# Second output stage of a decoder layer: its weights prepared during cross attention, low parts on GpSimd, scatters spread over two tiles

## Chip, cores and metric

One core of one Trainium2 chip. The metric is the device time of one execution in microseconds; the kernel before takes 2526.17 us, the median of 3 runs (2526.06 to 2526.66). All times below come from these runs and from one profiled execution of the kernel before.

## What is computed

A pre-norm decoder layer in float32 over 16 sequences of 112 tokens (1792 tokens of width 512): self attention with compressed keys and values, cross attention to 375 context tokens per sequence, then a mixture of experts.

```
x = x + self_attention(layernorm(x))              # 16 heads
x = x + cross_attention(layernorm(x), ctx) @ Wo.T # 16 heads of 128; Wo is (512, 2048)
x = x + moe(layernorm(x))

moe: probs = softmax(x @ classifier.T)            # 12 choices, 8 of them real experts
     top 2 of probs + bias; weight 1.5 * probs
     out  = sum of weight * (silu(x @ gate.T) * (x @ up.T)) @ down.T over chosen experts
          + x * (sum of the weights of the 4 choices without an expert)
```

The change touches the product with `Wo` that follows cross attention, what is computed with it (residual, norm, choice of experts, list of the tokens of each expert), and the cross attention ahead of it.

## The kernel before

The kernel runs stages one after the other; each is a block in which every engine has its own program in order, and a barrier stands between blocks. Every float32 product is made of three TensorE products: a value is split into a high part (rounded, made by a copy) and a low part (value minus high part), and hi*hi, hi*lo and lo*hi are summed in PSUM (`mm3`, L75 to L77).

`cross_attention` (block at 1024 to 1957 us) loops over 16 batches of four steps. In a step TensorE scores a quarter of the heads of batch b, weighs and projects keys and values of batch b+1; GpSimd's `project` adds and scales the next batch's keys and makes a low part of the context (L1957 to L1969); VectorE takes maxima and divides (L2220, L2227); ScalarE takes exponentials. The last batch has no next one to project, so GpSimd has nothing to do in it.

`cross_output` (1960 to 2228 us) is the second output stage. It goes over 14 tiles of 128 tokens. For tile t:

- SP loads the 16 heads' outputs in 4 chunks of 4 heads (L1486) and the residual (L1489), two tiles ahead, and stores the normed rows (L1494). A chunk is loaded when the low part of the tile before has been made of the same buffer (`o_lo_ready`).
- ScalarE makes the high part `o_hi` (`high`, L1562) when TensorE has used that chunk of the tile before; VectorE makes the low part `o_lo` (`low`, L1607).
- TensorE: `project` (4 chunks of 12 products, 128x512), `turn` (L1728, four transposes of the normed tile), `count` (L1747, L1748), `route` (12 small products). Its order for tile t is: project chunks 0 and 1 of t+1, turn t, project chunks 2 and 3 of t+1, count t-1, route t.
- VectorE: `norm` (residual added L1615, statistics L262 and L265, scaled L269), low part, `route(t-1)` (L1631 to L1649, the choice of two experts), `turn`, low part, `locate(t-2)` (L1659 to L1665, the places of the tile's tokens in the experts' lists), two low parts.
- GpSimd: `root(t)` (L275, L277: the variance to the power -0.5, which `norm` waits for), then `scatter(t-2)`: two indirect DMAs (L1540), one for the first and one for the second choice of each token. Each waits until the one before has landed (`scattered`), the first also for `locate(t-2)`.

`count(t-1)` on TensorE waits for `locate(t-2)` and `route(t-1)` of VectorE. `locate(t)` waits for the scatters of t-2.

Before the first tile the weights `Wo` come in 16 loads of one head each (L1499, 256 KB) through 8 buffers, ScalarE makes their high parts (L1587), VectorE their low parts (L1689), and the projection of tile 0 waits for each head (`w_lo_ready`). The classifier, the bias and the zeros of the lists are loaded ahead of them (L1476 to L1479). After the block comes `experts` (from 2228 us).

Of the kernel before, what the change touches and what calls it, by code (L numbers as in the profile page):

```python
# [11 lines left out]
ALU = mybir.AluOpType  # L12
# [1374 lines left out]
def cross_output(nc, oT, w_src, res, router, keep):  # L1387
# [4 lines left out]
    with ctx:  # L1392
# [3 lines left out]
        RAW = 8  # L1396
        w_raw = sb('w_raw', [P, RAW, D])
        w_hi = sb('w_hi', [P, H, D], F32R)
        w_lo = sb('w_lo', [P, H, D], F32R)
# [15 lines left out]
        w_in = [ctx.sem(f'w_loaded{i}') for i in range(RAW)]  # L1415
        w_hi_ready = ctx.sem('w_hi_ready')
        w_lo_ready = ctx.sem('w_lo_ready')
# [55 lines left out]
        def _(sp):  # L1473
            for i in range(2):
                y_put[i].open(sp)
            sp.dma_start(cls[:, :, :], cls_src).then_inc(r_src, 16)  # L1476
# [4 lines left out]
            def load(t, h, par, chunks=range(NQ), residual=True):  # L1481
                cols = bass.ds(t * P, P)
                for c in chunks:
                    if not isinstance(t, int) or t:
                        wait(sp, o_lo_ready, t, c - NQ)
                    sp.dma_start(o_raw[:, c, :, :], oT[:, c * HQ:(c + 1) * HQ, cols]).then_inc(o_in[c].sem, 16)  # L1486
                if residual:
                    wait(sp, added, t, -2)
                    sp.dma_start(r_in[par][:, :], res[cols, :]).then_inc(r_loaded[par].sem, 16)  # L1489
# [23 lines left out]
        def _(pool):  # L1513
            identity(pool, ident[:, :], id_ready)
            pool.iota(iota_i[:, :], pattern=[[1, TOTAL]], base=0, channel_multiplier=0).then_inc(id_ready, 1)
            pool.wait_ge(id_ready, 3)
            pool.tensor_copy(iota[:, :], iota_i[:, :]).then_inc(id_ready, 1)
            pool.memset(fill[:, :], 0).then_inc(zeroed, 1)
# [12 lines left out]
            exponent(pool, minus_half[:, :], half_ready)  # L1531

            def scatter(t, par):
                for c in range(2):
                    if c == 0:
                        wait(pool, p_step, t, 4)
                    if c or not isinstance(t, int) or t:
                        wait(pool, scattered, t, c - 1)
                    carry(pool, t, ticks)
                    pool.indirect_dma_start(tokens, bass.IndirectOffsetOnAxis(ap=dest_i[par][:, c:c + 1], axis=0), id_i[par][:, :], None).then_inc(scattered.sem, 16)  # L1540
            pool.wait_ge(list_ready, 16)
            for par in range(2):
                layer.root(pool, par, minus_half)

            def pair(h):
                for par in range(2):
                    layer.root(pool, h * 2 + par, minus_half)
                    scatter(h * 2 + par - 2, par)
            pair(1)
            with pool.Fori(2, TT // 2) as h:  # L1550
                pair(h)
            scatter(TT - 2, 0)
            scatter(TT - 1, 1)
            pool.wait_ge(scattered.sem, scattered.at(TT - 1, 1))

        @block.scalar
        def _(act):
# [16 lines left out]
            def body(t, h, par, ahead=True):  # L1574
                if ahead:
                    high(t + 2, 0)
                if not (isinstance(t, int) and t == 0):
                    route(t - 1)
                turn(t, h, par)
                if ahead:  # L1580
                    high(t + 2, 1)
                    high(t + 2, 2)
                if ahead:
                    high(t + 2, 3)
            for h in range(H):
                act.wait_ge(w_in[h % RAW], 16 * (h // RAW + 1))
                act.activation(w_hi[:, h, :], w_raw[:, h % RAW, :], ACT.Copy).then_inc(w_hi_ready, 1)  # L1587
                if h % HQ == 0:
                    high(0, h // HQ)
            for c in range(NQ):  # L1590
                high(1, c)
# [10 lines left out]
        def _(dve):  # L1602
            added.open(dve)

            def low(t, c):
                wait(dve, o_hi_ready, t, c)
                dve.tensor_tensor(o_lo[:, c, :, :], o_raw[:, c, :, :], o_hi[:, c, :, :], ALU.subtract).then_inc(o_lo_ready.sem, 1)  # L1607
# [59 lines left out]
            def body(t, h, par, ahead=True):  # L1667
                norm(t, h, par)
                if ahead:
                    low(t + 2, 0)  # L1670
# [3 lines left out]
                if ahead:  # L1674
                    low(t + 2, 1)
                if not (isinstance(t, int) and t < 2):
                    locate(t - 2, par)
                if ahead:
                    low(t + 2, 2)
                    low(t + 2, 3)  # L1680
# [6 lines left out]
            for h in range(H):  # L1687
                dve.wait_ge(w_hi_ready, h + 1)
# [1052 lines left out]
```

## Time and profile before

| | |
|---|---|
| Median of 3 runs | 2526.17 us (2526.06 to 2526.66) |
| Profiled execution | 2526.26 us, span 2524.6 us, mean granted TensorE clock 0.939 |
| TensorE matmul busy | 2182.0 us (86% of the span) |
| VectorE, ScalarE, GpSimd busy | 1332.6, 1030.3, 785.3 us (53%, 41%, 31%) |
| Low parts of the outputs on VectorE (L1607) | 56 of 0.691 us |
| Scatters on GpSimd (L1540) | 28, from 2020.3 to 2223.3 us |

The profile has a row per instruction: its engine, line, what it writes and reads, and the idle time of the engine before it with the instruction that ended it. The span is the time from the first to the last instruction; the execution's time is a little longer. A projection's row lasts 0.39 us at full clock, but the engine starts the next one before it ends, so distances of starts are read rather than durations.

### The profile page before, as it was taken

How to read it: one execution, taken by the hardware profiler on the slowest of the kernel's cores; microseconds unless marked ns; L12 is line 12 of the kernel's file. 1: busy time of each engine (PE TensorE's matmuls, PEld its weight loads, DVE VectorE, ACT ScalarE, POOL GpSimd, SP SyncE). 2: the span in 40 equal slices, each digit the busy share in tenths (PEclk: the TensorE clock that was granted, in tenths of full speed). 3: DMA queues.
4: the chain of work that ended last, by engine and by line, in shares of the span. 5: the costliest groups of instructions: out<-in, count | busy, mean ns of one | idle time of the engine just before them, and what ended most of it. 6: DMA issues, size and time to landing. Idle time of an engine off the chain costs nothing. (4 is left out here: it accounts for less than half of the span.)

```text
span 2524.6 us, 35645 instructions
## 1 busy us (share of the span) xinstructions
PE 2182.0 (86%) x10448; PEld 1661.2 (66%) x10448; DVE 1332.6 (53%) x2902; ACT 1030.3 (41%) x2200; POOL 785.3 (31%) x818
## 2 busy tenths in 40 slices
PE   5689999985898998599999999999998789638991
PEld 3588888864676776466666666666664667527771
DVE  3535555556667667354545454544544655534553
ACT  2323333334444344255555555555555311125660
POOL 2400000003555556432323232323230021145664
PEclk8899999997899999799999999999999999769995
DMA  7621221142344444212222222222211643154336
GB/s 283 166 73 37 63 66 36 33 164 88 107 126 136 134 121 147 87 54 65 73 67 67 64 57 64 57 70 66 74 32 37 193 97 94 38 193 132 104 104 191
DMA packets 291586, 243.77 MB, mean 97 GB/s; under 512 B 148034, under 2 KB 255026, under 8 KB 288562
## 3 DMA queue, kind: packets, MB, share of 16 engines
q1 hardware_dynamic: 271426, 194.38, 26.2%
q10 hardware_dynamic: 13584, 30.02, 3.3%
q0 software_dynamic: 6496, 18.37, 2.6%
q8 instruction: 41, 0.67, 0.1%
q14 instruction: 39, 0.32, 0.0%
HBM read 149.31 MB, written 93.42 MB: 96 GB/s over the span
## 5 line engine op out<-in xcount | busy, mean ns | idle before, releaser
L2220 DVE TENSOR_REDUCE ca_down<-ca_ps_s 112x1 f32<-112x487 f32 x256 | 164.6, 661 | 309.8 <-PE ca_ps_s L2035 307.3
L1963 POOL TENSOR_TENSOR ca_k<-ca_k 125x512 f32<-125x512 f32 x64 | 81.2, 1269 | 554.3 <-DVE ca_k L2205 554.3
L2035 PE MATMUL ca_ps_s<-ca_kT,ca_qT 128*112 128x487 f32 x512 | 230.5, 572 | 0.8 <-issue 0.8
L2124 ACT ACTIVATE ca_prob<-ca_ps_s,ca_down 112x487 f32<-112x487 f32 x256 | 169.8, 666 | 135.2 <-DVE ca_down L2220 131.1
L75 PE MATMUL out_ps_y<-out_w_hi,out_o_hi 128*128 128x512 f32 x448 | 191.8, 428 | 37.1 <-DVE out_w_lo L1288 19.0
L2051 PE MATMUL ca_ps_o<-ca_pT,ca_v 125*128 125x448 f32 (+1 forms) x512 | 203.2, 539 | 0.6 <-ACT ca_pT L2131 0.6
L75 PE MATMUL ca_ps_p<-ca_w_hi,ca_c_hi 128*125 128x512 f32 x384 | 174.1, 453 | 23.1 <-POOL ca_c_lo L1957 23.1
L76 PE MATMUL out_ps_y<-out_w_lo,out_o_hi 128*128 128x512 f32 x448 | 183.8, 410 | 0.0
L77 PE MATMUL out_ps_y<-out_w_hi,out_o_lo 128*128 128x512 f32 x448 | 183.5, 410 | 0.0
L2051 PEld LDWEIGHTS ca_ps_o<-ca_pT,ca_v 125*128 125x128 f32 (+1 forms) x512 | 97.1, 190 | 100.9 <-issue 100.1
L76 PE MATMUL ca_ps_p<-ca_w_lo,ca_c_hi 128*125 128x512 f32 x384 | 153.8, 400 | 0.0
L77 PE MATMUL ca_ps_p<-ca_w_hi,ca_c_lo 128*125 128x512 f32 x384 | 153.6, 400 | 0.0
L2042 PEld LDWEIGHTS ca_ps_t<-ca_ident,ca_prob 112*125 112x125 f32 x1024 | 131.6, 188 | 24.5 <-DVE ca_prob L2227 11.8
L599 POOL COPY sa_val<-lat_v 112x128 f32<-112x128 f32 (+1 forms) x64 | 18.9, 296 | 409.9 <-PE sa_ps_o L656 409.6
L2042 PE MATMUL ca_ps_t<-ca_ident,ca_prob 112*125 112x112 f32 x1024 | 132.9, 272 | 7.4 <-DVE ca_prob L2227 6.8
L75 PEld LDWEIGHTS out_ps_y<-out_w_hi,out_o_hi 128*128 128x128 f32 x448 | 90.4, 202 | 60.1 <-issue 33.6
L2131 ACT ACTIVATE ca_pT<-ca_ps_t 125x448 f32<-125x448 f32 x256 | 125.2, 543 | 4.3 <-PE ca_ps_t L2042 4.3
L2227 DVE TENSOR_SCALAR ca_prob<-ca_prob,ca_inv 112x487 f32<-112x487 f32 x256 | 121.2, 473 | 9.2 <-DVE ca_inv L2225 0.2
L75 PE MATMUL sa_ps_q<-sa_xh,qf_hi 128*128 128x448 f32 (+1 forms) x256 | 115.5, 451 | 8.4 <-DMA sa_xl<-x0T_lo 8.4
L2035 PEld LDWEIGHTS ca_ps_s<-ca_kT,ca_qT 128*112 128x112 f32 x512 | 80.4, 177 | 60.5 <-issue 60.5
L2202 DVE TENSOR_TENSOR ca_k<-ca_ps_p,ca_tab 125x512 f32<-125x512 f32 x64 | 44.3, 692 | 137.8 <-ACT ca_sq L2104 137.8
L707 ACT ACTIVATE sa_ov<-sa_ps_o 128x448 f32<-128x448 f32 x64 | 35.0, 547 | 196.9 <-PE sa_ps_o L656 187.8
(291 smaller groups left out, 5591.3 us busy)
## 6 DMA issues: line engine op xcount, KB each, us to landing
self_outT<-sa_ov SPq DMA_DIRECT2D x64, 224.0 KB, 2.4
out_o_raw<-self_outT SPq DMA_DIRECT2D x56, 256.0 KB, 3.0
cross_qT<-out_qt SPq DMA_DIRECT2D x56, 256.0 KB, 2.4
ca_qT<-cross_qT SPq DMA_DIRECT2D x64, 224.0 KB, 2.8
cross_outT<-ca_ov SPq DMA_DIRECT2D x64, 224.0 KB, 3.0
out_o_raw<-cross_outT SPq DMA_DIRECT2D x56, 256.0 KB, 3.5
ffn_raw<-in_expert_w SPq DMA_DIRECT2D x8, 1536.0 KB
ca_c_first<-in_ctxT SPq DMA_DIRECT2D x15, 750.0 KB, 5.1
```

Source lines behind the costliest of these rows:

```text
L75: pe.matmul(out, a_hi, b_hi, start=start, stop=False)
L76: pe.matmul(out, a_hi, b_lo, start=False, stop=False)
L77: return pe.matmul(out, a_lo, b_hi, start=False, stop=stop)
L1963: pool.tensor_tensor(k1[0:m, :], k1[0:m, :], k2[0:m, :], ALU.add).then_inc(k_added.sem, 1)
L2035: pe.matmul(ps_s[j % 2][:, :], qT[i % 2][:, j, :], kT[par][:, i, :], start=True, stop=True).then_inc(scored.sem, 1)
L2042: mm = pe.transpose(ps_t[j % 2][0:CT, t, :], prob[j][:, t * CT:(t + 1) * CT], ident[0:S, 0:S])
L2051: mm = pe.matmul(ps_o[:, :, :], v[par][0:M[t], t, i * HD:(i + 1) * HD], pT[i % 2][0:M[t], t, :, :], start=(t == 0), stop=(t == 3))
L2124: act.activation(prob[j][:, 0:KV], ps_s[j % 2][:, :], ACT.Exp, bias=down[:, j:j + 1], accum_out=total[:, j:j + 1]).then_inc(exped.sem, 1)
L2131: act.activation(pT[i % 2][0:CT, :, j, :], ps_t[j % 2][0:CT, :, :], ACT.Copy).then_inc(pT_ready.sem, 1)
L2202: dve.tensor_tensor(h4(k1[0:m, :]), h4(ps), over_heads(tab[par][0:m, i, 0, :], HQ), ALU.mult)
L2220: dve.tensor_reduce(down[:, j:j + 1], ps_s[j % 2][:, :], AX.X, ALU.max, negate=True).then_inc(maxed.sem, 1)
L2227: dve.tensor_scalar(prob[j][:, 0:KV], prob[j][:, 0:KV], inv[:, j:j + 1], None, ALU.mult).then_inc(probs.sem, 1)
```

## The change

- `CrossOutputWeights` holds the weights of the second output stage in two buffers of 16 heads at the right end of SBUF, with the raw weights in the place of the low parts. It is made before `cross_attention` and handed to it as `next_w`, then to `cross_output` as `ahead_of`.
- ScalarE issues four loads of 4 heads (1 MB) in batch 0 of cross attention, one at the head of each step. GpSimd splits one head (copy, then subtraction) at the end of each step of batches 1 and 14, and two in each step of batch 15.
- In `cross_output` the loads and splits of the weights, their semaphores and TensorE's waits on them are gone. SP's first issues are the outputs of tile 0. GpSimd's start is reordered around the low parts of tile 0.
- The low parts of the outputs are made by GpSimd.
- A tile's two scatters stand in different tiles of GpSimd's order: `root(t)`, second scatter of t-3, two low parts of t+2, first scatter of t-2, two low parts of t+2.
- ScalarE's `route(t-1)` stands before its first high part of t+2.

```diff
+class CrossOutputWeights(ExitStack):
+    def __init__(self, nc, w_src):
+        super().__init__()
+        self.src = w_src
+        with nc.sbuf_tensor("out2_w_raw", [P, H, D], F32, side="right") as self.w_raw:
+            pass
+        self.w_lo = self.enter_context(nc.sbuf_tensor("out2_w_lo", [P, H, D], F32R, side="right"))
+        self.w_hi = self.enter_context(nc.sbuf_tensor("out2_w_hi", [P, H, D], F32R, side="right"))
...
+    def load(self, eng, c):
+        heads = slice(c * HQ, (c + 1) * HQ)
+        eng.dma_start(self.w_raw[:, heads, :], self.src[:, heads, :]).then_inc(self.w_in[c], 16)
+
+    def split(self, pool, h):
+        pool.wait_ge(self.w_in[h // HQ], 16)
+        pool.tensor_copy(self.w_hi[:, h, :], self.w_raw[:, h, :]).then_inc(self.hi_ready, 1)
+        pool.wait_ge(self.hi_ready, h + 1)
+        pool.tensor_tensor(self.w_lo[:, h, :], self.w_raw[:, h, :], self.w_hi[:, h, :], ALU.subtract)
...
 cross_output, SP
+            load(0, 0, 0)
             sp.dma_start(cls[:, :, :], cls_src).then_inc(r_src, 16)
...
-            for h in range(H):
-                if h >= RAW:
-                    sp.wait_ge(w_lo_ready, h - RAW + 1)
-                sp.dma_start(w_raw[:, h % RAW, :], w_src[:, h, :]).then_inc(w_in[h % RAW], 16)
-                if h % HQ == 0:
-                    load(0, 0, 0, [h // HQ], h == H - HQ)
...
 cross_output, GpSimd
+            def low(t, c):
+                wait(pool, o_hi_ready, t, c)
+                carry(pool, t, ticks)
+                pool.tensor_tensor(o_lo[:, c, :, :], o_raw[:, c, :, :], o_hi[:, c, :, :], ALU.subtract).then_inc(o_lo_ready.sem, 1)
+
             identity(pool, ident[:, :], id_ready)
+            pool.memset(fill[:, :], 0).then_inc(zeroed, 1)
+            exponent(pool, minus_half[:, :], half_ready)
+            for c in range(NQ):
+                low(0, c)
...
+            def body(t, par, ahead=True):
+                early = lambda n: isinstance(t, int) and t < n
+                layer.root(pool, t, minus_half)
+                if not early(3):
+                    scatter(t - 3, 1, 1 - par)
+                if ahead:
+                    low(t + 2, 0)
+                    low(t + 2, 1)
+                if not early(2):
+                    scatter(t - 2, 0, par)
+                if ahead:
+                    low(t + 2, 2)
+                    low(t + 2, 3)
...
 cross_output, ScalarE
             def body(t, h, par, ahead=True):
+                if not (isinstance(t, int) and t == 0):
+                    route(t - 1)
                 if ahead:
                     high(t + 2, 0)
-                if not (isinstance(t, int) and t == 0):
-                    route(t - 1)
                 turn(t, h, par)
...
 cross_output, VectorE: low() and its calls removed
-            def low(t, c):
-                wait(dve, o_hi_ready, t, c)
-                dve.tensor_tensor(o_lo[:, c, :, :], o_raw[:, c, :, :], o_hi[:, c, :, :], ALU.subtract).then_inc(o_lo_ready.sem, 1)
...
 cross_attention, GpSimd
             def step(b, h, i, par, more):
                 if more:
                     project(b + 1, i, 1 - par)
+                if isinstance(b, int) and b:
+                    first = {1: i, B - 2: HQ + i, B - 1: 2 * (HQ + i)}[b]
+                    for head in range(first, first + (2 if b == B - 1 else 1)):
+                        next_w.split(pool, head)
...
 cross_attention, ScalarE
+                if isinstance(b, int) and b == 0:
+                    next_w.load(act, i)
                 exp(b, i, 0)
```

## Rows read from the trace of the kernel before

**Rows 1.** view of windows: us, busy us (instructions) per engine, clock, DMA share, GB/s.
```profile
1095.00:1895.00 800.00, 800.00 (x3434) 539.41 (x3434) 398.31 (x970) 414.87 (x957) 243.71 (x213) 1.00 0.23 62
...
1960.00:1985.00 25.00, 15.40 (x56) 11.07 (x57) 16.02 (x25) 15.12 (x24) 2.48 (x15) 0.80 0.90 279
...
2060.00:2100.00 40.00, 33.89 (x153) 27.43 (x152) 21.10 (x76) 7.89 (x18) 7.52 (x11) 0.89 0.38 87
```

**Rows 2.** waits, 2000 to 2200 us: engine line <- releaser: us, times, longest.
```profile
DVE out_yn L269 <- POOL out_mean_var L277: 59.8, 12, 7.2
...
PE out_ps_x L1728 <- DVE out_yn L269: 20.3, 9, 5.0
```

**Rows 3.** timeline of TensorE: start, us, line, operation, count, idle before.
```profile
1989.05 0.66 PE L1728 MATMUL out_ps_x<-out_ident,out_yn 128*128 128x128 f32 x4
...
2015.03 0.60 PE L1728 MATMUL out_ps_x<-out_ident,out_yn 128*128 128x128 f32 x4
...
2060.17 0.39 PE L75 MATMUL out_ps_y<-out_w_hi,out_o_hi 128*128 128x512 f32 x1
2060.40 0.39 PE L76 MATMUL out_ps_y<-out_w_lo,out_o_hi 128*128 128x512 f32 x1
...
2064.16 0.63 PE L75 MATMUL out_ps_y<-out_w_hi,out_o_hi 128*128 128x512 f32 x1
...
2080.12 0.65 PE L1728 MATMUL out_ps_x<-out_ident,out_yn 128*128 128x128 f32 x4 [2.25 <-DVE out_yn L269]
...
2180.83 0.60 PE L1728 MATMUL out_ps_x<-out_ident,out_yn 128*128 128x128 f32 x4
...
2193.61 1.12 PE L1728 MATMUL out_ps_x<-out_ident,out_yn 128*128 128x128 f32 x4 [5.00 <-DVE out_yn L269]
```

**Rows 4.** timeline of GpSimd, one tile of the second output stage.
```profile
2054.37 1.48 POOL L1540 DMA_INDIRECT tokens_of_experts<-out_id_i,out_dest_i  x1 [9.18 <-DVE out_dest_i L1665]
2060.39 0.96 POOL L1540 DMA_INDIRECT tokens_of_experts<-out_id_i,out_dest_i  x1 [4.54 <-DMA tokens_of_experts<-out_id_i,out_dest_i]
2061.37 0.25 POOL L275 TENSOR_SCALAR out_mean_var<-out_mean_var 128x1 f32<-128x1 f32 x1
```

**Rows 5.** timeline, start of the stage: SP's first issue, TensorE's first projection.
```profile
1960.86 0.36 SPq L1476 DMA_DIRECT2D out_cls<-in_clsT  x1
...
1968.47 0.77 PE L75 MATMUL out_ps_y<-out_w_hi,out_o_hi 128*128 128x512 f32 x1 [12.12 <-DVE out_o_lo L1607]
```

**Rows 6.** single lines (duration ns min/median/max), then timelines of GpSimd and VectorE.
```profile
L1957 POOL TENSOR_TENSOR ca_c_lo<-ca_c_first,ca_c_hi x48: 1148/1171/2742, 1027.0 to 1876.6; 128x500 fp32r<-128x500 f32 x48
...
2274.23 4.62 POOL L2388 TENSOR_TENSOR ffn_w_lo<-ffn_raw,ffn_w_hi 128x2048 fp32r<-128x2048 f32 x1 [5.44 <-ACT ffn_w_hi L2483]
...
2278.19 1.75 DVE L2586 TENSOR_TENSOR ffn_w_lo<-ffn_raw,ffn_w_hi 128x1024 fp32r<-128x1024 f32 x1 [1.90 <-ACT ffn_w_hi L2483]
...
2287.84 1.22 DVE L2586 TENSOR_TENSOR ffn_w_lo<-ffn_raw,ffn_w_hi 128x1024 fp32r<-128x1024 f32 x1 [1.92 <-ACT ffn_w_hi L2483]
```

**Rows 7.** timelines: VectorE's route and locate, first and last; a high part of ScalarE.
```profile
2064.03 0.16 DVE L1633 RECIPROCAL out_small<-out_small 128x1 f32<-128x1 f32 x1 [0.50 <-ACT out_prob L1572]
...
2070.03 0.17 DVE L1665 CAST out_dest_i<-out_dest 128x2 uint32<-128x2 f32 x1
...
2070.67 0.63 ACT L1562 ACTIVATE out_o_hi<-out_o_raw 128x512 fp32r<-128x512 f32 x1 [2.09 <-PE out_ps_y L77]
```

**Rows 8.** landing of L1486 and of L1540.
```profile
DMA to landing us min/median/max: 2.8/3.5/7.7
...
DMA to landing us min/median/max: 2.5/4.3/6.9
```

**Rows 9.** like loads of ScalarE; waits 1100 to 1956 us; last batch on TensorE.
```profile
L907 ACTq DMA_DIRECT2D out_wq_raw<-in_xwqT x4: 547/644/691, 552.3 to 558.9; - x4
...
ACT ca_prob L2124 <- DVE ca_down L2220: 127.6, 124, 1.3
...
1920.67 1.51 PE L2042 MATMUL ca_ps_t<-ca_ident,ca_prob 112*125 112x112 f32 x8 [1.44 <-DVE ca_prob L2227]
```

More of the change, by code:

```diff
@@ L1475, in _, with load, store @@
                 y_put[i].open(sp)
+            def load(t, h, par):
+                cols = bass.ds(t * P, P)
+                for c in range(NQ):
+                    if not isinstance(t, int) or t:
+                        wait(sp, o_lo_ready, t, c - NQ)
+                    sp.dma_start(o_raw[:, c, :, :], oT[:, c * HQ:(c + 1) * HQ, cols]).then_inc(o_in[c].sem, 16)
+                wait(sp, added, t, -2)
+                sp.dma_start(r_in[par][:, :], res[cols, :]).then_inc(r_loaded[par].sem, 16)
+            def store(t, h, par):
+                cols = bass.ds(t * P, P)
+                wait(sp, normed, t)
+                sp.dma_start(rows_n[cols, :], yn[par][:, :]).then_inc(y_put[par].sem, 16)
+            load(0, 0, 0)
             sp.dma_start(cls[:, :, :], cls_src).then_inc(r_src, 16)
@@ L1479, in _ @@
             sp.dma_start(tokens.rearrange('(p n) o -> p (n o)', p=P), fill[:, :]).then_inc(list_ready, 16)
[L1481 to L1489, printed above, removed]
-            def store(t, h, par):
-                cols = bass.ds(t * P, P)
-                wait(sp, normed, t)
-                sp.dma_start(rows_n[cols, :], yn[par][:, :]).then_inc(y_put[par].sem, 16)
-            for h in range(H):
-                if h >= RAW:
-                    sp.wait_ge(w_lo_ready, h - RAW + 1)
-                sp.dma_start(w_raw[:, h % RAW, :], w_src[:, h, :]).then_inc(w_in[h % RAW], 16)
-                if h % HQ == 0:
-                    load(0, 0, 0, [h // HQ], h == H - HQ)
             load(1, 0, 1)
@@ L1541, in _, with scatter @@
[L1541 to L1554, printed above, removed]
+            def scatter(t, c, par):
+                if c == 0:
+                    wait(pool, p_step, t, 4)
+                if c or not isinstance(t, int) or t:
+                    wait(pool, scattered, t, c - 1)
+                carry(pool, t, ticks)
+                pool.indirect_dma_start(tokens, bass.IndirectOffsetOnAxis(ap=dest_i[par][:, c:c + 1], axis=0), id_i[par][:, :], None).then_inc(scattered.sem, 16)
@@ new lines, in _ @@
+            pool.wait_ge(list_ready, 16)
+            for c in range(NQ):
+                low(1, c)
+            for t in range(4):
+                body(t, t % 2)
+            with pool.Fori(2, TT // 2 - 1) as h:
+                for par in range(2):
+                    body(h * 2 + par, par)
+            for par in range(2):
+                body(TT - 2 + par, par, ahead=False)
+            scatter(TT - 3, 1, 1)
+            for t in range(TT - 2, TT):
+                for c in range(2):
+                    scatter(t, c, t % 2)
@@ L1556, in _ @@
+            wait(pool, scattered, TT - 1, 1)
         @block.scalar
@@ L2685, in build @@
         keep = acc, oh, place, weight, run, rows_n, tokens
-        cross_output(nc, o2T, xwoT, x1, (clsT, bias), keep)
+        with cross_out_w:
+            cross_output(nc, o2T, cross_out_w, x1, (clsT, bias), keep)
         experts(nc, expert_w, *keep, rows_y, out_rows)
```

66 lines of the change are left out of this document (16 added, 50 removed).

## Prediction

> **What bounds the kernel now.** I read the table of windows first [rows 1], because shares over the whole span mix stages. From 1095 to 1895 us, cross attention, TensorE is busy 800.00 of 800.00 us at granted clock 1.00: nothing that only relieves another engine can gain there. The second output stage (1960 to 2228 us) is different. It opens with 15.40 busy us in 25, at a DMA share of 0.90, and from 2060 to 2100 TensorE is idle 6 of 40 us and the granted clock is 0.89.
>
> Next, who waits for whom in that stage [rows 2]. VectorE waits 59.8 us for GpSimd's root of the variance, and TensorE 20.3 us for the normed tile behind it. Only the second wait is a loss by itself; the first leads to it.
>
> The timeline of TensorE gives the price [rows 3]. `turn(t)` (L1728) is the tile's mark. It starts at 1989.05 (t=0), 2015.03 (2), 2080.12 (6), 2180.83 (12) and 2193.61 (13). The first two intervals together are 25.98 us, 12.99 each, with no idle time named before them; that is TensorE's own work. From t=6 to t=12 an interval is 16.79 us (100.71 in six). At t=6 2.25 us of it are idle time before `turn`, and behind such a wait a projection lasts 0.63 us (2064.16) instead of 0.39 (2060.17). That is the lower of the two clock levels, 1.2 GHz against 2.4: 512 columns then take 0.43 us from start to start, where 2060.17 to 2060.40 shows 0.23. What 16.79 has over 12.99 + 2.25, 1.55 us, is about eight such projections.
>
> The timeline of GpSimd names the cause [rows 4]. The scatter of a tile's first choice starts at 2054.37, the second can start only when the first has landed, at 2060.39, and `root` (L275) stands behind it at 2061.37. The variance had been ready long before. So the serial pair of scatters in front of `root` sets the pace, and TensorE pays for it twice, in idle time and in clock.
>
> **The change, part by part.** The sum is made against the profiled execution: 2526.26 us, of which 2524.60 are span and 1.66 around it; it stands 0.09 us above the median of 2526.17.
>
> *Start of the stage.* Removed from the stage: 16 weight loads, 16 splits on ScalarE and VectorE, and their waits. SP's first issue is at 1960.86 and the first projection at 1968.47 [rows 5]. Afterwards SP's first issue is the first chunk of the outputs. That load takes 2.8 us at best [rows 8], so it lands at 1963.7; ScalarE's high part 0.63 [rows 7], GpSimd's low part 1.2 (below), two handovers of 0.1: the first projection starts about 1965.7. The tile needs 72 projections before `turn(0)`: 7 at 0.43 and 65 at 0.227, 17.8 us, so `turn(0)` at 1983.4 rather than 1989.05: **-5.7 us**. Bounds: -2.8 (only the earlier start, the rest of the 20.6 us kept) and -7.1 (full clock at once). The identity, the zeros for the list and `exponent` are moved ahead of the low parts, the other tables behind them. The tables are eleven small instructions; at 0.2 us each (an estimate from `root`'s first one, 0.25 in rows 4) they end near 1971.6, behind four low parts that end near 1969.3, and tile 1's first low part is wanted only when the fourth chunk ends, at 1978. On SP the classifier, bias and list loads go behind five loads, some 2.5 us later, wanted by GpSimd near 1969: covered, and 1 us each if not.
>
> *A tile in the steady state.* VectorE loses four low parts; GpSimd takes them at about 1.2 us each (1.171 median for 128x500 [rows 6]), 4.8 us. With two scatters of about 1.0 and a `root` of 0.9 GpSimd holds 7.7 us of work per tile, below 13.1. What decides is the order. Let 0 be the end of the projections of tile t. ScalarE's last high part is ready at 0.9, the last low part stands before `root` until 2.2, VectorE's add and statistics, two passes over 512 columns at 0.7 (L2586 does 1024 in 1.22 [rows 6]) and a short one, are ready at 2.1; `root` ends at 3.15, the normed tile at 3.8. TensorE comes to `turn(t)` after count and route (1.6, what 12.99 leaves beside 48 projections and `turn`) and 24 projections (5.45), at 7.1. So the new wait in front of `root` has a margin of 3.3 us. Queued behind it on GpSimd: scatter of t-3's second choice (first one issued some 6 us earlier in the tile before), two low parts, scatter of t-2's first choice, two low parts. These low parts are wanted by TensorE some 8 us later, and they free the buffers for SP's loads of t+3, which land 3.5 us after issue [rows 8] and are wanted a tile later. ScalarE's `route`, now ahead of its first high part, holds that until 4.6, when the chunk is just used: nothing.
>
> On VectorE, `route(t-1)` and `locate(t-2)` follow. Their row distance, 2064.03 to 2070.20, is 6.17 us with one low part in it [rows 7]: 5.5 without. Starting at 4.5 they would end at 10.0, or 10.3 since `turn`'s result comes at 8.3. TensorE asks for them in `count` at 13.1. With nothing late the tile is TensorE's own again. I take 13.1 us, from the two undisturbed intervals of 12.99 on average (a little more, since `count` is missing in the first). Twelve intervals, t=0 to t=12: 157.2 instead of 191.78 (1989.05 to 2180.83): **-34.6 us**. Bounds: -35.9 (12.99 each) and -23 (14.1, see the rivals).
>
> *Does GpSimd's work hold VectorE back?* The subtraction L2586, 128x1024 with both inputs in SBUF, takes 1.22 us where GpSimd only issues a DMA, and 1.75 us where it starts at 2278.19 while GpSimd's subtraction runs until 2278.85 [rows 6]: it begins in effect when that ends (0.66 + 1.09). So I let `route` and `locate` be held by one low part each, up to 1.2 us: the chain ends at 11.7, still 1.4 before `count`. The Trainium skill, "SBUF — State Buffer", section "SBUF: two separate sides", speaks against this change: the two engines share a pair of SBUF ports as an exclusive lock, so a VectorE instruction with two SBUF inputs waits for the whole GpSimd instruction. By that rule the move could cost the lock rival's time below, without it the move is free; these rows agree with it.
>
> *Last tiles.* From t=12 to t=13 there is no further tile to project. Before: 12.78 us, 5.00 of them waiting for `root` behind two scatters [rows 3]. After: 0.6 + 5.45 to the end of the projections, 3.7 for the norm: 9.75. **-3.0 us** (bounds -4 and 0). From `turn(13)` on nothing changes: six scatters, each behind the landing of the last, to the end of the stage. In both versions six remain after `turn(13)`, the tenth tile's second one now standing before them behind `root`. **0**, within 2 us either way, as landings are 2.5 to 6.9 us.
>
> *Cross attention.* Four loads of 1 MB are issued by ScalarE in batch 0, 0.64 us each by the like loads L907 [rows 9]. ScalarE waits there for the maximum anyway (127.6 us in 124 times, about 1.0 each), and the DMA share is 0.23, so 4 MB over four steps of 14 us are covered: 0, with +2 as the other bound. GpSimd gets 16 splits of a copy (no row shows one of that size: more than the 0.25 of one column in rows 4, less than the 1.2 of a subtraction; I take 0.7) and a subtraction of 1.2: 2 us each. Batches 1 and 14 have one per step of about 14 us (933 us for 64 steps), behind the step's own work, and GpSimd is busy only 243.71 of 800 us [rows 1]: 0. In batch 15 eight stand in a row, some 16 us. TensorE is not full there, it waits for VectorE's `prob` (1.44 us at 1920.67 [rows 9]). Each first scaling of a pair can be held by up to 1.2 us, over one and a half steps: 0 to +6 if the clock falls too, I take **+1.5 us**. What covers the splits otherwise is TensorE's own work.
>
> Sum: 2526.26 - 5.7 - 34.6 - 3.0 + 1.5 = **2484.5 us**.
>
> **The rivals.** *The lock.* Were VectorE held three or four times a tile, its chain would end near 14.1 and `count` would wait 1 us in each tile: 12 x 1.0 = +12, 2496.5 us. For it: rows 6. Against: two of the four low parts fall where VectorE waits or reads PSUM.
>
> *The scatters stay serial.* Each still waits for the landing of the one before, two per tile. Their spacing within a tile is 6.0 us in rows 4, and may be as long as the longest landing, 6.9 [rows 8], twice which is 13.8, above 13.1. If the shorter tile crowds the DMA queues and spacing rises to 7.0, the period is 14.0: +11, 2495.5 us. Against it: the median landing of all 28 is 4.3 us [rows 8].
>
> *Slower than before.* The same chain decides from a period of 16.6 us on, a spacing of 8.3: 12 x 16.6 = 199 = 191.78 + 7.2, what the start, the last tile and cross attention save together. At 9 us the period is 18, 12 x 18 = 216, and the time 2484.5 + 58.8 = 2543 us. Against it: the longest landing seen is 6.9 us.
>
> *A wait takes the place of the one removed.* If `root` is as late as now because of the low parts before it (ScalarE's fourth high part late, for example), the period stays near 16 (191.78 us for twelve) and the last tile keeps its wait: 2526.26 - 5.7 + 1.5 = 2522 us, within 0.2%.
>
> *Cross attention pays more*, with the bound of +6: 2489 us.
>
> **How the numbers follow.** Forecast within 2479 to 2490: 0.62. Lock: 0.12. Serial scatters at 14: 0.12. Cross attention +6: 0.06. Period unchanged: 0.04. Slower: 0.04. All but the last two are faster by over 0.2% (5 us, about what a measurement of this kernel can tell from no change): 0.92; within it 0.04; slower 0.04. The low end adds the good bounds (-1.4, -1.3, -1, -1.5, and -2 of the last landings): 2477.3. The high end is either rival of +12 with +4.5 of cross attention: 2501.
>
> **What the profile after would show.** First L75 on `out_ps_y` at 1965 to 1966 plus what cross attention lost; `turn` every 13.0 to 13.3 us with no idle time before it and clock 1.00 from the second tile on; `root` no longer behind a landing; GpSimd's low part 1.2 us, stretched VectorE instructions beside it. The lock would show as TensorE's `count` waiting for `dest_i`; the serial chain as GpSimd's second scatter waiting for DMA in each tile and `turn` waiting for `yn`. The prediction is wrong if the interval of `turn` is over 14, or if batch 15 grows by more than 6 us.

## The result

The changed kernel takes 2491.23 us (median of 6 runs, 2486.19 to 2497.86); the kernel before, run beside it, 2524.34 (2521.97 to 2526.66). The ratio is 0.9872, 95% interval 0.9854 to 0.9891: 33 us faster. The forecast was 2484.5, range 2477 to 2501; the median lies in that range, 1.2 us above the band of 2479 to 2490 that had the chance 0.62. The profiled execution took 2492.17 us, 34.09 below the one of before.

First the view of windows, in the three stretches of [rows 1]: us, busy us (instructions) per engine, clock, DMA share, GB/s.

```profile
1095.00:1895.00 800.00, 800.00 (x3431) 539.71 (x3430) 397.97 (x970) 413.93 (x955) 258.26 (x230) 1.00 0.24 65
1960.00:1985.00 25.00, 15.49 (x55) 12.38 (x56) 1.37 (x4) 5.27 (x9) 11.97 (x23) 0.80 0.51 146
2060.00:2100.00 40.00, 40.00 (x204) 33.32 (x204) 24.20 (x77) 9.64 (x21) 24.61 (x24) 1.00 0.46 114
```

Cross attention carries GpSimd's splits and TensorE is as full as before. In the last line TensorE has lost its 6 idle us of 40 and the granted clock is 1.00, not 0.89. GpSimd has gone from 7.52 to 24.61 busy us. The waits from 2000 to 2200 us, against [rows 2]: engine line <- releaser: us, times, longest.

```profile
POOL tokens_of_experts L1560 <- DVE out_dest_i L1691: 36.3, 11, 5.6
DVE out_yn L269 <- POOL out_mean_var L277: 22.9, 12, 2.8
...
PE out_ps_c L1755 <- DVE out_dest_i L1691: 11.6, 3, 5.6
...
PE out_ps_x L1736 <- DVE out_yn L269: 1.8, 1, 1.8
```

VectorE waits 22.9 us for `root` instead of 59.8, TensorE 1.8 us for `yn` instead of 20.3. Of the three waits of `count` for `dest_i` two (5.56 and 5.19 us) lie behind the last turn, where nothing is left to project; the third, 0.82 us, is in the long tile below.

The turns in TensorE's timeline, against [rows 3]: start, us, line, operation, count, idle time before.

```profile
1989.02 0.60 PE L1736 MATMUL out_ps_x<-out_ident,out_yn 128*128 128x128 f32 x4
...
2055.87 0.49 PE L1736 MATMUL out_ps_x<-out_ident,out_yn 128*128 128x128 f32 x3
...
2069.33 0.60 PE L1736 MATMUL out_ps_x<-out_ident,out_yn 128*128 128x128 f32 x4
...
2109.71 0.60 PE L1736 MATMUL out_ps_x<-out_ident,out_yn 128*128 128x128 f32 x4
...
2125.80 0.60 PE L1736 MATMUL out_ps_x<-out_ident,out_yn 128*128 128x128 f32 x4
...
2152.71 0.49 PE L1736 MATMUL out_ps_x<-out_ident,out_yn 128*128 128x128 f32 x3
2162.41 0.67 PE L1736 MATMUL out_ps_x<-out_ident,out_yn 128*128 128x128 f32 x4 [1.80 <-DVE out_yn L269]
```

From `turn(0)` to `turn(12)` it is 163.69 us instead of 191.78. Ten of the twelve intervals are 13.45 or 13.46, the first is 13.01, and one, from 2109.71, is 16.09. So two things differ from the forecast of 13.1: every tile is 0.36 us longer, and one tile 2.6 more. The experiments are about these two, and about which part of the change brought what.

How the 34.09 us come together, both profiled executions: up to the end of cross attention +3.28 (3.24 of it are there at 1079.82 us, and the first of the new loads is issued at 1079.08); end of cross attention to the first projection -2.24; to `turn(0)` -1.07; twelve intervals -28.09; t=12 to 13 -3.08; `turn(13)` to the experts' first matmul -1.54; the rest -1.35. The stretches with unchanged code vary from profile to profile: cross attention ended between 1953.0 and 1964.5, the experts' stage took 273.7 to 282.8, the kernel before 2511.89 to 2531.00 in all. The usual intervals of `turn` repeat to 0.1 us, so the readings below go by them; the long ones do not repeat.

### The profile page after: what moved, and what is told of

Read it like the earlier page. It is cut to its first block and busy times, and to the rows that moved or that the text cites. A ratio compares the mean times of both kernels' runs of the same rounds, so it can differ in the third digit from the quotient of the medians.

```text
span 2490.5 us, 35704 instructions
## 1 busy us (share of the span) xinstructions
PE 2181.5 (88%) x10448; PEld 1664.9 (67%) x10448; DVE 1309.4 (53%) x2830; ACT 1020.9 (41%) x2184; POOL 887.9 (36%) x906
```

## Experiments: which part brings what

All kernels are read in the same way. "Start" is SP's first issue in the stage to `turn(0)`, "twelve" is `turn(0)` to `turn(12)`, "spacing" the mean distance from start to start of the projections at full clock, worked out from TensorE's timeline. "w-o" is the start of `w_hi` in its partition less that of `o_hi`, in bytes, modulo 512 (in all kernels it is the same for `w_lo` and `o_lo`). The last column is the ratio to the kernel before, run beside it. The last three kernels had one run each (2487.68, 2481.57 and 2488.29 us), so only their intervals are read; starts, spacings and intervals are always those of one profiled execution.

| kernel | low parts | scatters | weights | w-o | spacing | usual interval | twelve | start | ratio |
|---|---|---|---|---|---|---|---|---|---|
| before | VectorE | pair | in stage | 0 | 0.228 | 12.8 to 18.2 | 191.78 | 28.19 | 1 |
| changed | GpSimd | apart | ahead | 416 | 0.2345 | 13.46 | 163.69 | 24.72 | 0.9872 |
| a2_after_again | GpSimd | apart | ahead | 416 | 0.234 | 13.46 | 166.48 | 24.59 | 0.9896 |
| e1_apart_only | VectorE | apart | in stage | 0 | 0.228 | 13.16 | 158.14 | 27.79 | 0.9879 |
| e4_weights_only | VectorE | pair | ahead | 416 | 0.234 | 13.0 to 18.0 | 192.86 | 22.75 | 0.9971 |
| e2_low_dve | VectorE | apart | ahead | 416 | 0.2345 | 13.46 | 161.07 | 22.74 | 0.9844 |
| e3_pair | GpSimd | pair | ahead | 416 | 0.234 | 13.0 to 18.7 | 203.49 | 24.73 | 1.0039 |
| e5_pad32 | GpSimd | apart | ahead | 384 | 0.232 | 13.37 | 160.05 | 24.66 | 0.9858 |
| e8_place | VectorE | apart | ahead | 0 | 0.228 | 13.17 | 157.77 | 23.51 | 0.9842 |
| e12_place_gps | GpSimd | apart | ahead | 0 | 0.228 | 13.16 | 169.78 | 24.25 | 0.9873 |
| e10_out_shift | VectorE | apart | ahead | 448 | 0.233 | 13.41 | 160.55 | 23.89 | - |
| e11_w_shift | VectorE | apart | ahead | 0 | 0.228 | 13.17 | 157.60 | 23.56 | - |
| e13_both_shift | VectorE | apart | ahead | 0 | 0.228 | 13.16 | 157.66 | 22.37 | - |

(e6_warm, e8_place with extra projections, stands in its own section.)

**The scatters apart, alone.** The kernel before with this in place of `scatter(t-2)`:

```diff
 layer.root(pool, t, minus_half)
-scatter(t - 2, par)
+if not isinstance(t, int) or t > 2:
+    scatter(t - 3, 1, 1 - par)
+scatter(t - 2, 0, par)
```

> The kernel before with one part of the change only: GpSimd's order per tile is root(t), scatter of the second choice of t-3, scatter of the first choice of t-2. Weights are loaded and split inside the stage, low parts stay on VectorE, as before. Theory (the pair of scatters ahead of root set the pace, the rest is cover): the interval of turn falls from 16.79 us to 13.0 to 13.5, t=12 to t=13 from 12.78 to 9.8, the start of the stage is unchanged: 28 to 34 us less than before plus 3, so 31 to 37 us faster, ratio 0.985 to 0.988. If in addition the projections come at 0.227 us here (0.235 in the changed kernel), the slower spacing belongs to the moved weights or to GpSimd's low parts, and the interval is about 13.0. Rival (low parts on VectorE are the next bound, so both parts are needed): the interval stays above 14.5 and the gain is under 25 us. Rival (GpSimd's lock costs in the changed kernel): no interval over 14 here after tile 2, and the times of the runs lie within 1 us of each other.

Measured: 2489.43 us (2488.20 to 2495.11), ratio 0.9879 (0.9847 to 0.9910). Two tiles on TensorE:

```profile
2019.04 0.60 PE L1732 MATMUL out_ps_x<-out_ident,out_yn 128*128 128x128 f32 x4
2032.19 0.60 PE L1732 MATMUL out_ps_x<-out_ident,out_yn 128*128 128x128 f32 x4
2045.35 0.60 PE L1732 MATMUL out_ps_x<-out_ident,out_yn 128*128 128x128 f32 x4
```

and GpSimd in one tile, against [rows 4]:

```profile
2071.07 1.09 POOL L1539 DMA_INDIRECT tokens_of_experts<-out_id_i,out_dest_i  x1 [1.75 <-DMA tokens_of_experts<-out_id_i,out_dest_i]
2078.88 1.40 POOL L1539 DMA_INDIRECT tokens_of_experts<-out_id_i,out_dest_i  x1 [6.72 <-DVE out_dest_i L1669]
2081.31 0.22 POOL L275 TENSOR_SCALAR out_mean_var<-out_mean_var 128x1 f32<-128x1 f32 x1 [1.03 <-DVE out_mean_var L265]
```

`root` now waits for VectorE's variance, 1.03 us, and for no landing. This one part takes 33.6 us off the twelve intervals and 3.2 off the last tile, all that was forecast for the whole change there (34.6 and 3.0), and with this alone the kernel is as fast as the changed one. The low parts on VectorE are no bound: the rival that both parts are needed falls. The four runs spread over 6.9 us though GpSimd makes no low parts here.

**The weights ahead, alone.**

```diff
 # the changed kernel, low parts back on VectorE
-scatter(t - 3, 1, 1 - par)
 scatter(t - 2, 0, par)
+scatter(t - 2, 1, par)
```

> One part of the change alone: the weights are loaded and split beside cross attention and the stage starts with the outputs' chunks; the low parts stay on VectorE and a tile's two scatters stay together, ahead of the next root, as before. Theory: SP's first issue to the first projection falls from 7.6 to 4.5, first projection to turn(0) from 20.5 to 18.2, so 5 us less at the start; the twelve intervals stay what the pair of scatters makes them, 190 to 195 us, a little more by the slower projections (12 x 0.3 = 3.6 us where TensorE sets the pace, nothing where the scatters do); sum 2516 to 2522, 2 to 7 us faster than before. Rival (weights at the right end cost in every tile what the start gains): within 2 us of before.

Measured: 2514.34 us (2510.18 to 2520.50, 10 runs), ratio 0.9971 (0.9956 to 0.9987), a little below the 2516 to 2522 expected. The start is 5.4 us shorter, what the prediction had put down (5.7); the twelve intervals are 192.86, as long as before.

**The scatters together again, low parts on GpSimd.**

```diff
 # the changed kernel, GpSimd
-scatter(t - 3, 1, 1 - par)
 low(t + 2, 0); low(t + 2, 1)
 scatter(t - 2, 0, par)
+scatter(t - 2, 1, par)
 low(t + 2, 2); low(t + 2, 3)
```

> The changed kernel with both scatters of a tile together again: root, two low parts, both scatters of t-2, two low parts. Theory (apart is what counts): GpSimd stands at the second scatter until the first has landed (about 5 us), and the low parts behind it and the next root come late: interval 15.5 to 17, time 2515 to 2530. Rival (the low parts between are room enough, or the weights ahead are what counts): interval 13.5 to 14, time 2490 to 2497.

Measured: 2531.74 us, ratio 1.0039 (1.0025 to 1.0054), slower than before and above the 2515 to 2530 expected; the usual interval is near 18 us, not 15.5 to 17, and the twelve together take 203.49 us. GpSimd's timeline shows why:

```profile
2073.05 1.09 POOL L1560 DMA_INDIRECT tokens_of_experts<-out_id_i,out_dest_i  x1 [4.90 <-DVE out_dest_i L1689]
2077.61 0.96 POOL L1560 DMA_INDIRECT tokens_of_experts<-out_id_i,out_dest_i  x1 [3.47 <-DMA tokens_of_experts<-out_id_i,out_dest_i]
2078.59 2.52 POOL L1531 TENSOR_TENSOR out_o_lo<-out_o_raw,out_o_hi 128x512 fp32r<-128x512 f32 x2
2081.07 0.23 POOL L275 TENSOR_SCALAR out_mean_var<-out_mean_var 128x1 f32<-128x1 f32 x1
```

A landing, and then 2.52 us of low parts, stand ahead of `root`. So low parts on GpSimd are no gain of their own: in this order they cost 10.6 us against e4_weights_only (203.49 against 192.86), from which e3_pair differs by them and by ScalarE's order.

## Experiments: the long tile

**Low parts back on VectorE.**

```diff
-# GpSimd: low(t + 2, c), four times a tile
+# VectorE: norm(t); low(t + 2, 0); route(t - 1); turn(t); low(t + 2, 1); locate(t - 2); low(t + 2, 2); low(t + 2, 3)
 # ScalarE
-route(t - 1); high(t + 2, 0)
+high(t + 2, 0); route(t - 1)
```

> The changed kernel with the low parts of the outputs back on VectorE (in the places they had before, ScalarE's route again behind the first high part). Theory: GpSimd's low parts buy nothing once the scatters are apart, and cost an interval of 16 us now and then, because VectorE's small instructions are held behind them: here no interval over 14, runs within 1 us of each other, and the time is that of the fastest runs of the changed kernel or up to 3 us below, 2483 to 2487 (ratio 0.983 to 0.985). The spacing of the projections tells whether GpSimd's low parts slow TensorE: 0.227 us if so, 0.235 if it is the place of the weights. Rival (VectorE needs the relief): interval over 13.6 in every tile, time 2492 or more.

Measured: 2482.00 us (2476.00 to 2490.46), ratio 0.9844 (0.9805 to 0.9883). No interval is above 13.46, and the start is 2 us shorter. The time is 1 us below the range expected. The spread of the runs is 14 us, where 1 was expected, so GpSimd's low parts alone don't make the runs spread; where the spread arises was not traced run by run. The spacing stays 0.2345, so GpSimd's work isn't what slows the projections either.

**The changed kernel again.**

> The changed kernel itself, on the chip of the other kernels of this group. It tells which of its readings come back: interval 13.46 with a projection spacing of 0.2345 us in every ordinary tile (both kernels with the weights at the right end and without extra tile showed exactly that), first projection to turn(0) 19.5, SP's first issue to the first projection 5.2. Theory (GpSimd's low parts now and then collide with VectorE's chain): at least one interval above 13.6 again, in another tile. Rival (the 16.09 was a single accident): all twelve near 13.46, total 161.1.

Measured: 2494.11 us (2489.51 to 2496.22), ratio 0.9896 (0.9880 to 0.9913). Nine of the twelve intervals within 13.02 and 13.46, and three long ones: 14.53, 14.41 and 16.84. The last of them, GpSimd first, then VectorE, then TensorE:

```profile
2070.09 1.09 POOL L1560 DMA_INDIRECT tokens_of_experts<-out_id_i,out_dest_i  x1 [2.41 <-DMA tokens_of_experts<-out_id_i,out_dest_i]
2071.21 2.56 POOL L1531 TENSOR_TENSOR out_o_lo<-out_o_raw,out_o_hi 128x512 fp32r<-128x512 f32 x2
2078.57 0.98 POOL L1560 DMA_INDIRECT tokens_of_experts<-out_id_i,out_dest_i  x1 [4.79 <-DVE out_dest_i L1691]
```

```profile
2070.24 0.17 DVE L1666 CAST out_best_f<-out_best_i 128x8 f32<-128x8 uint32 x1
2070.45 3.37 DVE L1668 TENSOR_SCALAR out_hot<-out_iota,out_best_f 128x12 f32<-128x12 f32 x1
```

```profile
2077.72 0.39 PE L1755 MATMUL out_ps_c<-out_chosen,out_below 128*128 128x8 f32 x2 [1.58 <-DVE out_dest_i L1691]
```

L1668 works on 12 columns and lasts about 0.2 us; here it lasts 3.37, until 2073.82, and GpSimd's two low parts end at 2073.77. One instruction of VectorE was held until the end of the second of two GpSimd low parts, which ran back to back because the scatter in front of them had waited 2.41 us for a landing. By its row it began 0.76 us before the first of them, beside that scatter. Then the chain closes: `locate` is late, `count` waits 1.58 us, GpSimd's next scatter waits 4.79 us for the destinations, and the low parts and `root` behind it are late as well. In the changed kernel's first profile the tile from 2109.71 is the same: low parts back to back (2.69 us), L1666 1.92 and L1668 1.47 us, `count` waiting 0.82 (in this tile L1666 ended with the first low part and L1668 with the second), and behind it about seven projections at the lower clock level:

```profile
2119.56 0.63 PE L77 MATMUL out_ps_y<-out_w_hi,out_o_lo 128*128 128x512 f32 x1
2119.99 0.63 PE L75 MATMUL out_ps_y<-out_w_hi,out_o_hi 128*128 128x512 f32 x1
...
2122.29 0.40 PE L75 MATMUL out_ps_y<-out_w_hi,out_o_hi 128*128 128x512 f32 x1
```

**GpSimd's low parts at the other place of the weights.** To have this without the other effect, the changed kernel was given the weights' place of e8_place (next section). The two then differ by the engine of the low parts, and by ScalarE's `route` and first high part, which stand in the other order.

```diff
 self.src = w_src
+self.enter_context(nc.sbuf_tensor("out2_w_pad", [P, 232], F32, side="right"))
```

> The changed kernel, low parts on GpSimd, with the same 928 bytes of padding as e8_place: against e8_place it differs by GpSimd's low parts alone, against the changed kernel by the place of the weights alone. Theory: ordinary intervals 13.16 with spacing 0.228, SP's first issue to turn(0) 24 us against 23 in e8_place (GpSimd's low part 1.3 us against 0.6), and now and then an interval of 14.5 to 17 where two low parts run back to back and hold one small instruction of VectorE for 2 us or more; total 2482 to 2492, on average 4 us above e8_place. Rival (GpSimd's low parts cost nothing at this place): no such interval, total within 1.5 us of 2480.7.

Measured: 2492.02 us (2485.47 to 2494.81), ratio 0.9873 (0.9854 to 0.9892), against 2480.73 (2479.66 to 2481.70), ratio 0.9842 (0.9825 to 0.9858) in e8_place. Nine intervals are between 12.75 and 13.17; three are 15.45, 18.17 and 18.12. The twelve together are 12.0 us above e8_place (169.78 against 157.77) and the medians 11.3 apart, more than the 4 expected. At the start of the second long one the rows of GpSimd and VectorE are

```profile
2067.26 1.09 POOL L1561 DMA_INDIRECT tokens_of_experts<-out_id_i,out_dest_i  x1 [2.12 <-ACT out_o_hi L1599]
2068.39 2.55 POOL L1532 TENSOR_TENSOR out_o_lo<-out_o_raw,out_o_hi 128x512 fp32r<-128x512 f32 x2
```

```profile
2067.71 3.27 DVE L1667 CAST out_best_f<-out_best_i 128x8 f32<-128x8 uint32 x1
2071.01 0.37 DVE L1669 TENSOR_SCALAR out_hot<-out_iota,out_best_f 128x12 f32<-128x12 f32 x2
```

Again the small instruction ends with the second low part (2070.98 and 2070.94) and begins beside the scatter ahead of the first. From 1990 to 2165 us, small instructions of VectorE's `route` and `locate` (24 columns or fewer) that last over 0.7 us are 11 in the changed kernel, 13, 12, 11 and 15 in a2, e5, e3 and e12, the kernels with low parts on GpSimd, and none in the nine others. Each of them ends within 0.2 us of the end of a GpSimd low part. That is shown. A single instruction held just before `turn`, for up to 2.1 us, lengthened no tile. The seven long intervals are those in which, from the start of `turn` on, one instruction was held over 3.2 us or two were held, 2.4 us or more together: none in e5_pad32, one, three and three in the others with the scatters apart.

## Experiments: the projections' spacing

The other 0.3 us per tile. 48 projections at 0.2345 instead of 0.2277 are 0.33 us, the whole difference between 13.46 and e1's 13.16. It is there in all ordinary tiles of every kernel with the weights at the changed kernel's place, also in e2_low_dve, where GpSimd has no low parts.

```diff
 self.src = w_src
+self.enter_context(nc.sbuf_tensor("out2_w_pad", [P, 8], F32, side="right"))
```

> The changed kernel with a tile of 32 bytes per partition at the right end of SBUF ahead of the weights, nothing else: w_hi moves from byte 163808 to 163776 of its partition and w_lo from 196576 to 196544, so both begin at a multiple of 64 bytes, as they do before the change (64576 and 97344). Theory (TensorE streams the weights slower from an odd multiple of 32 bytes): the projections' spacing falls from 0.235 to 0.227 us, an ordinary interval of turn from 13.46 to about 13.05, and the time by 14 x 48 x 0.0085 = 5.7 us, to 2480 to 2486 (ratio near 0.985). Rival (the place of the weights doesn't matter; the spacing comes from something else, such as the outputs' tiles, GpSimd's work or the right end as such): spacing 0.235, time 2487 to 2497 as without the tile.

Measured: 2487.94 us (2478.91 to 2490.44), ratio 0.9858 (0.9821 to 0.9895), spacing 0.232, interval 13.37. Expected by the theory was 0.227, and by the rival 0.235: multiples of 64 bytes are not the rule, but the place matters, since 32 bytes changed the spacing. So I looked at where the operands begin. In the kernel before `w_hi`, `w_lo`, `o_hi` and `o_lo` have all the same remainder modulo 8192; in the changed one they don't. 928 bytes of padding (the line of e12_place_gps, here in e2_low_dve) bring that back.

> The kernel with the low parts on VectorE and the scatters apart (e2_low_dve), and 928 bytes per partition of padding at the right end of SBUF, so that w_hi starts at byte 162880 and w_lo at 195648: both then have the same remainder by 8192 (7232) as o_hi (56384) and o_lo (64576), which is so in the kernel before as well (w_hi 64576, w_lo 97344, o_hi 138304, o_lo 146496, all 7232). Theory (what counts is the place of moving and stationary operand relative to each other or to a block of up to 8192 bytes): spacing 0.2277 and interval 13.16 as in e1_apart_only, so 3.6 us less over twelve intervals than e2_low_dve, about 2478 us. Rival (the right end as such, or the order of outputs below weights, is slower): spacing 0.232 to 0.235, interval 13.38 to 13.46, about 2482 us.

Measured as the theory had it: spacing 0.228, intervals 13.15 to 13.28 after a first one of 12.75; in all 2480.73 us, where about 2478 was expected. One tile of e2_low_dve, then one of e8_place, which differ by nothing but the padding:

```profile
2027.05 0.60 PE L1738 MATMUL out_ps_x<-out_ident,out_yn 128*128 128x128 f32 x4
2040.51 0.60 PE L1738 MATMUL out_ps_x<-out_ident,out_yn 128*128 128x128 f32 x4
```

```profile
2029.12 0.60 PE L1739 MATMUL out_ps_x<-out_ident,out_yn 128*128 128x128 f32 x4
2042.29 0.60 PE L1739 MATMUL out_ps_x<-out_ident,out_yn 128*128 128x128 f32 x4
```

Three more kernels say what of the place counts; each is e8_place with one or two of the tiles moved:

```diff
 # e10_out_shift, and e13_both_shift
+sb('o_pad', [P, 16])
 o_raw = sb('o_raw', [P, NQ, HQ, P])
 # "out2_w_pad": [P, 232] in e8_place and e10_out_shift, [P, 360] in e11_w_shift, [P, 216] in e13_both_shift
```

> e8_place with 64 bytes of padding ahead of the outputs' tiles: o_hi moves from byte 56384 to 56448 and o_lo from 64576 to 64640, w_hi and w_lo stay (162880, 195648). Only the remainders of the stationary operand and the moving one by 8192 differ now, by 64. Theory (the two operands' places relative to each other count): spacing of the projections 0.230 to 0.235, interval 13.25 or more. Rival (only the weights' own place counts, where a run of 2048 bytes begins in its block): 0.228 and 13.16 as in e8_place.

Outputs 64 bytes on: spacing 0.233, interval 13.41, slower though the weights haven't moved.

```profile
2032.81 0.60 PE L1740 MATMUL out_ps_x<-out_ident,out_yn 128*128 128x128 f32 x4
2046.22 0.60 PE L1740 MATMUL out_ps_x<-out_ident,out_yn 128*128 128x128 f32 x4
```

> e8_place with the padding at the right end 512 bytes longer: w_hi at byte 162368 and w_lo at 195136, outputs' tiles as in e8_place. The remainders by 8192 differ by 512 from those of the outputs, those by 512 are all 64 as before. Theory (the block that counts is 512 bytes or less): 0.228 and 13.16. Rival (it is larger): 0.230 to 0.235 and 13.25 or more. With e5_pad32, whose remainders by 512 were 448 for the weights and 64 for the outputs and which had 0.2324, the two together say how fine the rule is.

Weights 512 bytes off: 0.228 and 13.17. The block is 512 bytes or less.

> e10_out_shift, where the outputs' tiles stood 64 bytes off, with the weights moved by the same 64 bytes: o_hi at byte 56448, o_lo at 64640, w_hi at 162944, w_lo at 195712, all with the remainder 128 by 512. Theory (the places of the two operands relative to each other count): interval 13.16 and spacing 0.228, as in e8_place. Rival (each operand's own place counts, 64 by 512 being a good one): interval 13.38 to 13.46 and spacing 0.232 to 0.235.

Both 64 bytes off: 0.228 and 13.16. This one, a single run, tells the two readings apart: with both moved the spacing is back, so the difference of the two counts and not either operand's own place.

```profile
2041.92 0.60 PE L1740 MATMUL out_ps_x<-out_ident,out_yn 128*128 128x128 f32 x4
2055.11 0.60 PE L1740 MATMUL out_ps_x<-out_ident,out_yn 128*128 128x128 f32 x4
```

Six kernels of the table with the difference 0 modulo 512 have 0.228 (the kernel before is one of them), and the differences 384, 416 and 448 have 0.232, 0.2345 and 0.233. What in the hardware does it, and what a smaller block such as 128 bytes would show, stays open.

## Experiment: the clock at the start

```diff
 used.open(pe)
 turned.open(pe)
+for i in range(10):
+    pe.matmul(ps_y[1][:, :], w_hi[:, i, 0:P], w_hi[:, i, :], start=True, stop=True)
 pe.wait_ge(id_ready, 2)
```

> e8_place with ten extra projections ahead of the stage, w_hi by w_hi into the second output bank, which the first real projection of tile 1 overwrites; they wait for nothing and run while SP's first loads are on their way. Theory (the first projections are slow because TensorE has been idle for nearly 10 us before them): the extra ones run at 0.43 us each, 4.3 us, beside the loads; behind them the first real projections run at 0.23, and first projection to turn(0) falls from 18.2 to about 16.8: 1.4 us less than e8_place. Rival (the clock falls again in the gap between, or the first projections wait for outputs rather than for the clock): no change. If the extra ones are not over when the first chunk is ready, up to 1 us is given back.

Measured: 2480.97 us (2472.92 to 2484.62), ratio 0.9846 (0.9829 to 0.9863), in total not told apart from e8_place. In the stage it can be:

```profile
1957.91 4.11 PE L1723 MATMUL out_ps_y<-out_w_hi 128*128 128x512 f32 x10 [4.89 <-PEq L126]
1962.20 0.47 PE L75 MATMUL out_ps_y<-out_w_hi,out_o_hi 128*128 128x512 f32 x1 [0.18 <-DVE out_o_lo L1623]
1962.51 0.39 PE L76 MATMUL out_ps_y<-out_w_lo,out_o_hi 128*128 128x512 f32 x1
```

The first real projections start 0.31 and then 0.23 us apart, `turn(0)` comes 16.44 us behind them (expected 16.8), and the start is 20.96 us instead of 23.51 in e8_place. The slow projections were the clock after TensorE's idle time (9.16 us in e8_place, 4.89 before the ten extra ones here), and not a wait. How many there are varies: 12 in each of the five profiles with low parts on GpSimd, 5, 6, 11, 11, 11 and 5 in e2, e4, e8, e10, e11 and e13.

## Why the prediction was right, and where its steps were off

**What bounds the kernel** was read rightly. The pair of scatters in front of `root` was the pace, and e1_apart_only gives the whole step of -34.6 and -3.0 back as -33.6 and -3.2 with nothing else changed.

**Start of the stage, forecast -5.7, measured -3.5** (28.19 to 24.72). The earlier first projection is nearly as forecast, 5.2 us after SP's first issue instead of 4.8. Mis-sized was the term "7 projections at 0.43": 12 were slow, 5 x 0.2 = 1.0 us, and the faster ones came at 0.235, 0.5 us over 60. With the low parts on VectorE the start is shortened by 4.3 to 5.8 us.

**A tile, forecast 13.1, measured 13.46.** The step that was off is the sentence that the tile is TensorE's own again "from the two undisturbed intervals of 12.99": these were measured with the weights in another place. The prediction priced what was moved in time and not what was moved in SBUF. Twelve tiles at 0.36 are 4.3 us, 3.6 of them (0.30 each) the spacing. The other 0.06 is in the average itself: the two intervals were 12.82, without `count`, and 13.16, which is also e1_apart_only's.

**The lock, forecast as a cover of 1.2 us per chain.** Here the forecast was half right. Direction and mechanism came as in [rows 6], and the stretched instructions are there, but I took one low part per held instruction; the traces show one instruction held for two in a row (3.27 and 3.37 us) and a chain held twice (1.92 + 1.47). That is more than was covered, in one tile of twelve in the first profile, three in the second, three in e12. One of the prediction's own signs of being wrong, an interval over 14, thus came in these tiles and not in the others. By the rule of the Trainium skill, "SBUF — State Buffer", section "SBUF: two separate sides", whichever engine holds the shared ports keeps them for its whole instruction. The traces agree in that every stretched row ends with a low part of GpSimd. They show more in the three holds of 3.2 to 3.4 us (3.37 in a2_after_again, 3.27 and 3.23 in e12_place_gps), where the waiting VectorE instruction did not get its turn between GpSimd's two; in the changed kernel's first profile it did (L1666). By their rows these three also began before the first low part, so which engine's row starts first did not decide.

The lock rival, with 2496.5 us, was thus the better description of the mechanism in single tiles (`count` waiting for `dest_i`), not of every tile. The rival of serial scatters did not come about: the median landing of the stage's first 23 scatters rose from 4.3 to 5.4 us (of all 28, from 4.3 to 5.1), and GpSimd waits 22.4 us for landings in all, but beside the lock no tile is longer for it. It does prepare the long tiles, since the scatter that waits pushes the low parts together. (Ahead of some of the pairs the trace names ScalarE's high part for that wait, but what this scatter waits for in the program is the landing of the one before.)

**Last tile, -3.0: -3.08. Tail, 0 within 2: -1.54.** Both right; the tail was 46.8 to 48.1 us in all the other kernels, 47.0 and 47.7 in e3_pair and e4_weights_only, which have the order of before, and 49.3 in before's one profile, so that difference isn't the change's. **Cross attention, +1.5: 0.** TensorE is 800.00 of 800.00 us busy, and from 1079.82 us to the end of the stage 0.04 us were lost. That it came out at nothing is one pair of profiles. GpSimd's copy took 0.61 us (forecast 0.7), the subtraction 1.27 (1.2):

```profile
1908.53 1.30 POOL L1410 TENSOR_TENSOR out_w_lo<-out_w_raw,out_w_hi 128x512 fp32r<-128x512 f32 x1
1909.77 0.61 POOL L1408 CAST out_w_hi<-out_w_raw 128x512 fp32r<-128x512 f32 x1
```

Together the steps gave -41.8 and the profile -34.1: short by 2.4 at the start and 6.5 in the tiles (163.69 against 157.2), 3.2 of unchanged code that came out longer, less 1.5 in cross attention and 2.9 in the tail and behind it.

**A version that beats both:** e8_place, 2480.73 us, ratio 0.9842 (0.9825 to 0.9858): scatters apart, weights ahead, low parts left on VectorE, the weights placed at the outputs' remainder modulo 512. Its twelve intervals are 5.9 us below the changed kernel's and its range of runs lies wholly below the latter's.

## What to carry to other kernels

When a trace shows an engine held by a chain of landings, move first only what stands in that chain, and test it alone: here one reordering gave nearly all, and relieving VectorE, which was no bound, cost more than it gave. GpSimd instructions that read two SBUF tiles are cheap beside VectorE only while they don't come in pairs against a chain of small VectorE instructions. When operands of TensorE are given a new place, compare the spacing of the matmuls before and after, and line the two operands up again.

## What was not expected of the hardware

- The spacing of matmuls at 128x512 in this data type went with the distance between the starts of moving and stationary operand, modulo 512 bytes: 0.228 us at 0, 0.232 to 0.2345 at 384 to 448.
- A VectorE instruction of 8 to 12 columns was held 3.2 to 3.4 us, from beside a scatter to the end of the second of two GpSimd subtractions of 1.27 in a row.
- After about 9 us of idle time TensorE's first projections ran at 0.43 us (1.2 GHz), 5 to 12 of them in otherwise like kernels; ten extra matmuls in the idle time made the real ones start at 0.23.
